# What carries the wait: a memset and a one-element product, or a semaphore increment

## The reference

```python
q = (xn @ Wq).reshape(b, n, H, DH).transpose(0, 2, 1, 3) * scale      # xn = layernorm(x)
k, v = one key and one value head, each with a null key and a null value in front
sim = jnp.einsum('bhid,bjd->bhij', q, k) + bias                       # bias: 16 x 512 x 513
sim = jnp.where(causal_mask, neg, sim)
sim = jnp.where(mask_p[:, None, None, :], sim, neg)
attn = jax.nn.softmax(sim, axis=-1)
out = jnp.einsum('bhij,bjd->bhid', attn, v) ... @ Wo
return layernorm(out, g_out)
```

## Time and profile before

| | us |
|---|---|
| median of three runs | 1868.44 |
| the profiled execution | 1867.34 |
| its span | 1865.6 |
| attention, 288 to 876 us of the span | 588.0 |
| PE busy in attention | 557.8 |
| DVE busy in attention | 431.3 |
| POOL busy in attention | 401.9 |
| memset at line 711, 512 times | 30.2 |
| product at line 682, 256 times | 46.9 |

### The profile page before, as it was taken

One profiled execution on the slowest core, in us unless ns is written; L12 is line 12 of the kernel. 1 busy time (PEld: TensorE's weight loads), 2 busy tenths in 40 slices (PEclk: granted clock), 3 DMA queues, 4 the chain that ended last, 5 costly groups with the idle time before them and its releaser, 6 DMA issues. The chain is left out here.

```text
span 1865.6 us, 37638 instructions
## 1 busy us (share of the span) xinstructions
PE 1684.3 (90%) x10388; PEld 1370.2 (73%) x10389; DVE 1032.4 (55%) x3158; ACT 721.2 (39%) x1883; POOL 773.9 (41%) x1460
## 2 busy tenths in 40 slices
PE   6899967999999999997888887969999999879998
PEld 5677755887877877876777776757777788658886
DVE  5444545786776776876544554643333343345555
ACT  2222215676676766765222211103333333311221
POOL 1000326676586675774445553032222222143323
PEclk9999997999998998998899998989999999989999
DMA  6566659797787887792544334024446633244423
GB/s 219 188 230 216 215 174 247 176 223 169 171 211 174 183 203 154 200 215 81 175 135 135 130 130 157 0 90 148 174 142 263 219 101 110 83 146 134 147 90 113
DMA packets 220232, 301.83 MB, mean 162 GB/s; under 512 B 15185, under 2 KB 128385, under 8 KB 218066
## 3 DMA queue, kind: packets, MB, share of 16 engines
q1 hardware_dynamic: 189970, 235.20, 44.1%
q0 software_dynamic: 11280, 35.99, 6.6%
q10 hardware_dynamic: 18864, 29.38, 4.6%
HBM read 187.26 MB, written 113.26 MB: 161 GB/s over the span
## 5 line engine op out<-in xcount | busy, mean ns | idle before, releaser
L785 ACT ACTIVATE probs<-scores,lowest 128x514 f32<-128x514 f32 (+3 forms) x512 | 281.9, 554 | 25.6 <-DVE lowest L712 24.9
L684 POOL TENSOR_SCALAR probs<-probs,rsums 128x512 f32<-128x512 f32 (+3 forms) x512 | 265.0, 524 | 0.0
L712 DVE CUSTOM_DVE_ANT_0 scores<-psum,resident 128x514 f32<-128x514 f32 (+3 forms) x512 | 245.6, 489 | 24.5 <-issue 19.1
L838 PE MATMUL psum<-ident,probs 128*128 128x128 f32 x1280 | 248.7, 293 | 9.6 <-POOL probs L684 9.3
L827 PE MATMUL psum<-keys,queries 128*128 (+4 forms) x640 | 229.1, 367 | 27.9 <-DMA queries_and_ones<-q_hi_d 19.5
L854 PE MATMUL psum<-probsT,v_now 128*64 128x128 f32 x2560 | 204.6, 290 | 10.1 <-DVE probsT L726 6.8
L838 PEld LDWEIGHTS psum<-ident,probs 128*128 128x128 f32 x1280 | 149.3, 143 | 63.7 <-issue 34.5
L827 PE MATMUL psum<-keys_lo_and_mask,queries_and_ones 128*128 (+4 forms) x640 | 191.3, 308 | 0.0
L793 ACT ACTIVATE probsT<-psum 128x128 f32<-128x128 f32 (+3 forms) x256 | 111.9, 437 | 185.4 <-PE psum L838 183.2
L854 PEld LDWEIGHTS psum<-probsT,v_now 128*64 128x64 f32 x2560 | 139.1, 140 | 52.9 <-issue 34.5
L726 DVE COPY probsT<-psum 128x128 f32<-128x128 f32 (+3 forms) x256 | 125.1, 489 | 85.2 <-PE psum L838 80.6
(11 more groups left out here) (242 smaller groups left out, 3802.0 us busy)
## 6 DMA issues: line engine op xcount, KB each, us to landing
ys_d<-y_out ACTq DMA_DIRECT2D x72, 256.0 KB, 2.1
q_hi_d<-q_hi SPq DMA_DIRECT2D x64, 256.0 KB, 2.6
q_lo_d<-q_lo SPq DMA_DIRECT2D x64, 256.0 KB, 3.0
queries<-q_hi_d SPq DMA_DIRECT2D x32, 512.0 KB, 5.3
queries<-q_lo_d SPq DMA_DIRECT2D x32, 512.0 KB, 7.5
queries_and_ones<-q_hi_d SPq DMA_DIRECT2D x32, 512.0 KB, 9.3
oT_d<-o_out SPq DMA_DIRECT2D x64, 256.0 KB, 5.4
o_in<-oT_d SPq DMA_DIRECT2D x32, 512.0 KB, 4.0
```

Of the source, the lines that this page charges most:

```text
L684: pool.tensor_scalar(out=row, in0=row, scalar1=rsums[:, n % RING:n % RING + 1], scalar2=1.0, op0=ALU.mult, op1=ALU.mult).then_inc(probs_sc ...
L712: dve.tensor_tensor_reduce(out=scores[n % 4][:, 0:CK[i]], in0=score_psum(i, n), in1=bias_of(resident, i, h), scale=1.0, scalar=3.0e38, op0 ...
L785: act.activation(probs[n % RING][:, 0:CK[i]], scores[n % 4][:, 0:CK[i]], ACT.Exp, bias=lowest[:, n % 4:n % 4 + 1], scale=-1.0, accum_out=s ...
L838: last = pe.transpose(probsT_bank[n % 2][:, j * P:(j + 1) * P], probs[n % RING][:, AHEAD + j * P:AHEAD + (j + 1) * P], ident[:])
```

## The change

On DVE the memset at line 711 is replaced by an instruction that increments a new semaphore `bias_begun`. Both waits are attached to it, so the separate wait instruction of line 710 is gone too, except where the sequencer computes a register in the same place. On POOL the product at line 682 is replaced by an increment of a new semaphore `scaling_begun`, with the one wait attached. Nothing waits for either of the new semaphores. Such an increment is carried out by the engine's sequencer; the engine itself gets no instruction. The tile `waited` is gone, and the buffers behind it lie 32 bytes lower in each partition. PE, ACT and SP have the same instructions in the same order. The memsets and products of the same kind elsewhere (line 672 in the same stage, and those of the other stages) stay.

```diff
-        waited = sb("waited", [1, 4])
...
+        bias_begun, scaling_begun = sem("bias_begun"), sem("scaling_begun")
...
                 if n % 2 == 0:
                     pool.wait_ge(rsums_ready, PB * b + n // 2 + 1)
-                    pool.tensor_tensor(out=waited[:, n // 2 % 4:n // 2 % 4 + 1], in0=ident[0:1, 0:1], in1=ident[0:1, 0:1], op=ALU.mult)
+                    pool.sem_inc(scaling_begun, 1)
                 row = probs[n % RING][:, AHEAD:CK[n // H]]
                 pool.tensor_scalar(out=row, in0=row, scalar1=rsums[:, n % RING:n % RING + 1], scalar2=1.0,
...
                 if not (isinstance(b, int) and b == 0 and n < 4):
 
                     dve.wait_ge(probs_ready, UB * b + n - 3)
-                dve.memset(spare["dve"][:, n % 2:n % 2 + 1], 0.0)
+                dve.sem_inc(bias_begun, 1)
                 dve.tensor_tensor_reduce(out=scores[n % 4][:, 0:CK[i]], in0=score_psum(i, n), in1=bias_of(resident, i, h),
```

## The result

The changed kernel takes 1873.67 us in the median of twelve runs (1870.49 to 1878.62), the kernel before 1867.78 us in twelve (1862.21 to 1870.42). The ratio is 1.0033, with a 95% interval of 1.0020 to 1.0045: slower by about 6 us, where 0.1% faster was forecast and the range ended at 1873.0. The profiled executions lie under these medians, by 2.3 us (after) and 0.4 us (before), and differ by 4.0 us.

A forecast was written before the change was run, and what follows sets the result against it. PE, busy 90% of the span, was taken to bound the kernel. POOL's -1.9 us and the late bias's +0.2 us gave -1.7 us on 1867.34 us, thus 1865.6, or 1866.7 us for the median; range 1861 to 1873 us.

The forecast's parts named there:

- What bounds: In attention PE sets the pace, busy 557.8 of 588 us; POOL's 193.1 us idle at line 682 are no cost.
- POOL's term, -1.9 us: Line 682: without the product the scaling starts 0.12 to 0.17 us earlier; 13 PE waits x 0.145 us gained.
- DVE's memsets, zero: Line 711: removing 512 memsets, 30.2 us of engine time, gains zero to 0.06 us a unit, taken as zero.
- DVE's late bias, +0.2 us: Line 712: the sequencer's wait starts late biases 0.08 us later; only the stage's start passes it on, 3 x 0.08 us.
- The second rival: Block 0 of each entry: PE feels biases 0.08 us late, 1876.7 us, or 1871.6 if half counts; chance 0.13.
- The loop's end, "I count zero": DVE's loop end, idle 509.54 to 512.16: the memset's 0.06 us give way to the increment's own time, counted zero.
- What would show it wrong: Attention: shorter 0.17 us PE waits, DVE idle ahead of line 712 up several us, or granted clock moved 0.01 or more.
- Several signs of being right: Attention: POOL busy about 355 us, DVE 402 to 431, PE's bias wait within 0.5 us, scaling 0.08 to 0.12 us after inverse.

The follow-up runs named there:

- the old place: The change on DVE alone with 66 idle increments ahead of DVE's first bias, its loop head back at instruction 632, against the kernel before: 1870.39 us, ratio 1.0004.
- the experiment with 66 increments: The changed kernel with 66 idle semaphore increments on DVE in front of its first bias, against the kernel before: 1865.09 us, ratio 0.9976.

## Why the prediction was wrong, point by point

**What bounds.** Right. PE sets the pace in attention, and what moved the time shows in its waits: 5.3 us more in sum for DVE and POOL. POOL's idle time grew from 193 to 234 us, which is no cost.

**POOL's term, -1.9 us.** The mechanism was right and the size of its unit wrong. PE waits in 13 pieces for POOL where 14 were forecast, but the scaling follows the inverse by 0.20 us, 0.05 us earlier than before, not 0.12 to 0.17. I took the price of a sequencer wait from DVE (0.12 us), whose row begins behind an arithmetic step of the sequencer, and used it on another engine. 13 x 0.05 is 0.7 us; the sum of PE's waits fell by 2.6 us in the one profile, 0.6 us of it for a DMA that landed earlier; the rest isn't accounted for. Alone it was worth 0.03%, not distinguishable from nothing.

**DVE's memsets, zero.** Right as far as can be measured: at the old place the removal on DVE alone gives 1.0004 (0.9993 to 1.0015), and written out, on top of POOL's half, 1842.8 against 1844.3 us, with intervals that overlap. Their 30 us lay beside other work of DVE: its busy time didn't fall.

**DVE's late bias, +0.2 us.** The unit was too small, 0.22 - 0.05 = 0.17 us instead of 0.08. It hardly mattered: with the pause away, DVE's half of the change costs 0.04% (-0.07% to 0.15%). The second rival, slower through this delay, would have given the right sign and nearly the right time (1871.6 to 1876.7 us) for a wrong reason; the experiment with 66 increments refutes it.

**The loop's end, "I count zero".** This is the step that failed. I read the earlier trace rows for what the memset adds there, 0.06 us, and took the 2.6 us of idle time as given. I asked what each removed instruction costs and not what its absence does to where the others lie. 66 instructions less ahead of the loop moved the end of a fetched block to 14 instructions behind the head, and that cost DVE 1.2 to 1.3 us in each of five returns. Measured by the starts of the biases, the changed kernel falls back by 1.4 to 1.7 us around each of the five, 7.9 us in all, and wins back 4.0 us in the rest of attention; that leaves the 3.9 us of the profiled execution. The medians differ by 6 us.

**What would show it wrong.** The text named DVE's idle time ahead of line 712 and a changed clock. The idle time came ahead of line 726, five times in one place, and the mean clock went from 0.952 to 0.949 (0.94 in attention both times). Several signs of being right failed too: in attention DVE was busy 436.9 us (402 to 431 forecast), POOL 364.3 (about 355), PE's wait for the bias grew by 1.2 us (at most 0.5), and the starts after inverse and scores took 0.20 and 0.22 us (about 0.12 at most).

## What to carry to other kernels

A change of the number of instructions moves the code behind it, and in front of a hardware loop that can cost or gain more than the instructions themselves. Before a small difference is put down to an edit, run a second version with idle instructions that restore the loop head's place. If an engine shows idle time for nothing that the profile names just behind a loop's return, try shifting the head or writing the loop out; here writing it out on all engines gave 1.4%.

## What the runs showed of the hardware

- DVE's loop body of 386 to 444 instructions stood still at each return: 2.7 to 3.3 us between the branch and the next instruction in nearly all kernels, 3.7 us where the head was the first instruction of a block. ACT's body, 325 rows of the trace, took 3.3 to 4.6 us. The instruction packets of 8192 bytes that come behind each return say that code was fetched again.
- It is not the length alone. POOL's body of 165 rows came back in 0.2 us. PE's is longer than DVE's, 827 rows of weight loads and sequencer steps in an entry with the matmuls not counted, and came back in 0.06 us. A second instruction queue, with packets of 16384 bytes, moved none from 433 to 814 us in the changed kernel, while the loop ran.
- DVE's blocks are 128 instructions long as far as these runs tell: 128 increments change nothing, 62 in the kernel before do the same as 66 fewer instructions in the other (62 + 66 = 128), and with blocks of 64 the kernel before would have had a block's end 12 instructions behind its head, where it shows no pause. Packets of 8192 bytes fit this, with the 64 bytes that an instruction has by the Trainium skill (Perfetto Trace Analysis, The 4-stage abstract model).
- With all entries of the changed kernel written out, DVE's longest idle time in attention that the profile puts down to nothing was 0.5 us.
- An increment with the wait attached took 21 ns of DVE's sequencer with one wait and 50 ns with two; where nothing else held it, the engine's next instruction began 127 ns after its end. On POOL it took 17 ns, and the next instruction began 150 ns after its end.
